# Issuing the down-projection weight loads from GpSimd's queue in place of SyncE's, in an eight-core transformer layer

## The chip, the cores and the metric

One Trainium2 chip, all 8 NeuronCores, one launch. Every core runs the same program on its own share of the tokens, and no core waits for another. The time is device microseconds of the slowest core.

## The reference

One post-norm transformer layer on x of shape (4, 4096, 2048): multi-head self-attention with 16 heads of 128, a projection, a residual and a layer norm, then a gated feed-forward network with 4-bit weights (I = 5632), an RMS norm of its result, a residual and a layer norm.

```python
x = _layernorm(x + attn(x, Wqkv, Wproj, bproj))
gate, up = x @ w_gate.T, x @ w_up.T        # w_* dequantized from fp4, group scales
y = (silu(gate) * up) @ w_down.T
y = y / sqrt(mean(y * y) + 1e-6)
x = _layernorm(x + y)
```

## The kernel before

The work is split by batch row and half of the sequence: each core has 2048 tokens. Three phases follow each other, each closed by waits for all of the one before.

Phase A computes Q, K, V and the attention, and between these dequantizes the packed weights into two scratch tensors in HBM, `wgu_scr` (gate and up) and `wdn_scr` (down, 5632 x 2048 bf16). Phase B does the projection, the residual and the first norm; it leaves h1 in HBM, once as f32 rows (`h_scr`) and once transposed (`h1T_scr`).

Phase C, in which the change lies, is the feed-forward network. It runs over 4 chunks (`ch`) of 512 tokens. A chunk has

- a gate-up stage: for each of 44 blocks `op` of 128 hidden units, 16 + 16 matmuls of 128x512 (L966 gate, L972 up) with the weight block `wbC` (1 MB, 4 buffers) and the chunk's transposed input `h1tc` (2 MB, 2 buffers); ScalarE does silu (L985), VectorE the product into `hffnT` (L994);
- two down stages (`pp` = 0, 1), each for a pair of 128-token tiles: for each of 44 blocks `ic`, 8 matmuls of 128x512 (L1040) with the weight block `wdC` (128 rows of 4 KB, 512 KB, 4 buffers) into all eight PSUM banks. All of `wdn_scr` is read once for each pair, 8 times in all;
- after each down stage an epilogue for each of its two tiles, on VectorE with two square roots on ScalarE: PSUM to `yC` (L1057), statistics, the residual with `h1rC` (L1103), the norm into `outfC` (L1136), and a store of 1 MB (L1145).

The order is that in which each engine's queue is written; there is no planner. SyncE's queue (SPq) issues all loads of phase C, in this order in a chunk: `h1tc` (L935), 44 times `wbC` (L947), then for each pair two loads of 1 MB `h1rC` (L1008) and 44 loads `wdC` (L1020). Each waits on SPq before it is issued: `wbC` number kc for the matmuls of kc-4 (L946), `h1rC` of a tile for the whole epilogue of the tile two before (`cyt`, L1007), `wdC` number kd for the last matmul of kd-4 (`dm`, L1019). So on SPq the loads `wdC` of pair 1 stand behind the epilogues of pair 0, and the loads of the next chunk stand behind the last `wdC` of this one.

GpSimd's queue (POOLq) issues in phase C only the 16 stores of `out` (L1145), each after its epilogue's last step. GpSimd computes nothing there.

TensorE starts the first block of a pair when `wdC` is there and the earlier pair's last tile has been copied out of PSUM (`cyev`); it starts a chunk's gate-up stage when the tile before the last one has been copied out. Its operation `op` waits for the product `op`-2 (`chm`), because gate and up use two pairs of banks in turn.

Of the kernel before, what the change touches and what calls it, by code (L numbers as in the profile page):

```python
# [111 lines left out]
def build_nc(cfg):  # L112
# [29 lines left out]
    d_wdn = nc.dram_tensor("wdn_scr", [I, H], BF16, kind="Internal").ap()  # L142
# [26 lines left out]
    with contextlib.ExitStack() as TOP:  # L169
        ET = TOP.enter_context  # L170
        sems = {n: ET(nc.semaphore(n)) for n in SEM_NAMES}
# [731 lines left out]
        with contextlib.ExitStack() as SC:  # L903
# [4 lines left out]
            wdC = [EC(nc.sbuf_tensor(f"wdC{i}", [128, H], BF16)) for i in range(4)]  # L908
# [10 lines left out]
            def phaseC(w: W):  # L919
# [10 lines left out]
                for ch in range(NTC):  # L930
                    if w.on("sync"):
                        s = w.eng
                        if ch >= 2:
                            s.wait_ge(sems["sCg"], w.m(f"cgc{ch-2}", "sCg"))
                        w.pinc(s.dma_start(out=h1tc[ch % 2][:],  # L935
                                           in_=d_h1T[:, ch * TOKCH:(ch + 1) * TOKCH]
# [3 lines left out]
                    for op in range(ITC):  # L940
                        par = op % 4
                        kc = ch * ITC + op
                        if w.on("sync"):
                            s = w.eng
                            if kc >= 4:
                                s.wait_ge(sems["sCg"], w.m(f"cg{kc-4}", "sCg"))  # L946
                            w.pinc(s.dma_start(out=wbC[par][:],  # L947
                                               in_=d_wgu[op, :, :].rearrange("(hc p) o -> p hc o",
                                                                             p=128)), "sCw", kc, 4)
# [3 lines left out]
                        par = op % 4  # L953
# [46 lines left out]
                    for pp in range(NPAIR):  # L1000
                        for tt2 in range(ntt2):
                            tt_abs = ch * TT + pp * 2 + tt2
                            parq = tt_abs % 2
                            if w.on("sync"):
                                s = w.eng
                                if tt_abs >= 2:
                                    s.wait_ge(sems["sCy"], w.m(f"cyt{tt_abs-2}", "sCy"))  # L1007
                                w.pinc(s.dma_start(out=h1r[parq][:],  # L1008
                                                   in_=d_h1[tt_abs * 128:(tt_abs + 1) * 128, :]),
# [3 lines left out]
                        for ic in range(ITC):  # L1013
                            kd = (ch * NPAIR + pp) * ITC + ic
                            par = ic % 4
                            if w.on("sync"):
                                s = w.eng
                                if kd >= 4:
                                    s.wait_ge(sems["sDm"], w.m(f"dm{kd-4}", "sDm"))  # L1019
                                w.pinc(s.dma_start(out=wdC[par][:],  # L1020
                                                   in_=d_wdn[ic * 128:(ic + 1) * 128, :]),
                                       "sDw", kd, 4)
                            else:
                                w.pnote("sDw", kd, 4)
                            for tt2 in range(ntt2):
                                for oc in range(NOC):
                                    if w.on("tensor"):
                                        t = w.eng
                                        if tt2 == 0 and oc == 0:
                                            w.pwait("sDw", kd, 4)  # L1030
                                            if ic == 0:
                                                t.wait_ge(sems["sCh"], w.c("sCh"))
                                                prev_last_tile = ch * TT + pp * 2 - 1
                                                if prev_last_tile >= 0:
                                                    t.wait_ge(sems["sCy"],
                                                              w.m(f"cyev{prev_last_tile}", "sCy"))
                                        lhs = (hffnT[:, ic, pp * 256 + tt2 * 128:
                                                     pp * 256 + (tt2 + 1) * 128] if TT > 1
                                               else hffnT[:, ic, 0:128])
                                        inst = t.matmul(pC[tt2 * 4 + oc][:, 0:OCW], lhs,  # L1040
                                                        wdC[par][:, oc * OCW:(oc + 1) * OCW],
                                                        start=(ic == 0), stop=(ic == ITC - 1))
                                        if tt2 == ntt2 - 1 and oc == NOC - 1:
                                            w.inc(inst, "sDm", 1)
                                    elif tt2 == ntt2 - 1 and oc == NOC - 1:
                                        w.note("sDm", 1)
                            w.snap(f"dm{kd}", "sDm")
                        for tt2 in range(ntt2):
                            tt_abs = ch * TT + pp * 2 + tt2
                            parq = tt_abs % 2  # L1050
                            if w.on("vector"):
# [4 lines left out]
                                for oc in range(NOC):  # L1056
                                    w.inc(v.tensor_copy(out=yC[:, oc * OCW:(oc + 1) * OCW],  # L1057
                                                        in_=pC[tt2 * 4 + oc][:, 0:OCW]),
# [4 lines left out]
                            if w.on("vector"):  # L1063
# [4 lines left out]
                                for st2 in range(NST):  # L1068
                                    last = v.bn_stats(out=sttC[:, st2, :],
                                                      in_=yC[:, st2 * STW:(st2 + 1) * STW])  # L1070
# [3 lines left out]
                                                     in_=sttC[:].rearrange("p a b -> p (a b)")),  # L1074
# [21 lines left out]
                            if w.on("vector"):  # L1096
# [13 lines left out]
                                for st2 in range(NST):  # L1110
                                    last = v.bn_stats(out=sttC[:, st2, :],
                                                      in_=r2[:, st2 * STW:(st2 + 1) * STW])
# [3 lines left out]
                                                     in_=sttC[:].rearrange("p a b -> p (a b)")),  # L1116
# [25 lines left out]
                            if w.on("gpsimd"):  # L1142
                                gp = w.eng
                                gp.wait_ge(sems["sCy"], w.c("sCy"))
                                w.pinc(gp.dma_start(out=d_out[tt_abs * 128:(tt_abs + 1) * 128, :],  # L1145
                                                    in_=outf[parq][:]), "sOut", tt_abs)
# [5 lines left out]
                if w.on("gpsimd"):  # L1152
                    for sname in ("sOut0", "sOut1"):
                        if w.c(sname) > 0:
                            w.eng.wait_ge(sems[sname], w.c(sname))

            run_phase(phaseC)

    return nc
# [65 lines left out]
```

## Time and profile before

| | us |
|---|---|
| median of the runs (2 runs, 6547.95 to 6553.09) | 6550.52 |
| profiled execution | 6540.59 |
| its span on the slowest core (core 1) | 6539.0 |
| spans of the eight cores | 6518.7 to 6539.0 |
| phase C begins at about | 4383 |

The profile is of core 1 of the profiled execution, and all times in rows are from its span's start. The mean granted clock of TensorE lies between 0.886 and 0.889 of its full speed on all cores. The profiled execution is 9.9 us below the median of the runs.

### The profile page before, as it was taken

Reading aid. Unit: us, or ns where it says so; the run is one execution under the profiler, and the core shown is the slowest. Engines: PE = TensorE matmul, PEld = TensorE weight load, DVE = VectorE, ACT = ScalarE, POOL = GpSimd, SP = SyncE. Lnnn points to the kernel's source line nnn. Section 1 sums busy time; section 2 is a strip of 40 time slices with the busy share of each in tenths; the row PEclk is TensorE's granted clock in tenths of the full one; section 3 lists DMA queues with packets and bytes.
Section 4 is the critical chain, followed back from the end, with each engine's and each line's share of the span. In section 5 each row is a group of like instructions: output and inputs, shape, how many; then the busy total and the mean of one; then the engine's idle time right before and its main releaser. Section 6 shows DMA issues by size and latency. Waiting matters only on the chain.

```text
span 6539.0 us, 82502 instructions; the slowest of 8 cores (6518.7 to 6539.0 us)
## 1 busy us (share of the span) xinstructions
PE 4668.7 (71%) x27520; PEld 2300.4 (35%) x27520; DVE 2362.7 (36%) x9935; ACT 2039.9 (31%) x2442; POOL 423.2 (6%) x510
## 2 busy tenths in 40 slices
PE   0587667876668776678766244449979979978995
PEld 0233443334443344433343122224434433433442
DVE  1234775347773367633576211111012112011003
ACT  0234765337663366733566111110000000000000
POOL 0000111001110011100111000000000000000000
PEclk9988898988988888999889677769989989989997
DMA  2333112341123321133111322234575466467565
GB/s 68 102 94 102 37 42 60 88 123 39 39 58 90 108 58 36 38 97 107 41 36 37 126 74 77 77 110 155 177 237 178 161 221 210 155 202 237 153 211 181
DMA packets 281821, 725.90 MB, mean 111 GB/s; under 512 B 26689, under 2 KB 43457, under 8 KB 271169
## 3 DMA queue, kind: packets, MB, share of 16 engines
q1 hardware_dynamic: 242306, 575.37, 28.2%
q0 software_dynamic: 39104, 145.27, 7.6%
q8 instruction: 231, 3.78, 0.2%
q14 instruction: 180, 1.47, 0.1%
HBM read 600.99 MB, written 119.54 MB: 110 GB/s over the span
## 4 chain that ended last, share of the span: by engine, by line
PE 47%; DMA 20%; DVE 15%; ACT 11%; issue 6%; POOL 0%; DVEq 0%; ACTq 0%; SPq 0%; POOLq 0%
DMA xf<-xt 10%; PE pC L966 9%; PE pC L972 9%; PE pC L1040 7%; ACT Pt L613 5%; PE pCV L514 5%; PE pCV L634 5%; PE pB L815 4%; PE pS L550 3%; DMA wdC<-wdn_scr 3%; PE pS L587 3%; DVE dqf L344 3%; DVE dq_bits L333 2%; ACT xbf L466 2%; DMA wq_st<-wqkvT 2%
## 5 line engine op out<-in xcount | busy, mean ns | idle before, releaser
L613 ACT ACTIVATE Pt<-pS,bias_c 128x1024 bf16<-128x1024 f32 x1024 | 1099.7, 1115 | 370.3 <-PE pS L587 359.4
L634 PE MATMUL pCV<-V_wave,Pt 128*128 128x129 bf16 x8192 | 706.5, 235 | 573.8 <-ACT Pt L613 315.1
L634 PEld LDWEIGHTS pCV<-V_wave,Pt 128*128 128x128 bf16 x8192 | 553.5, 105 | 1048.5 <-issue 1044.2
L1040 PE MATMUL pC<-wdC,hffnT 128*128 128x512 bf16 x2816 | 632.4, 383 | 197.4 <-DMA wdC<-wdn_scr 188.1
L514 PE MATMUL pCV<-wq_bf,xbf 128*128 128x512 bf16 x2048 | 521.7, 420 | 297.8 <-ACT V_wave L527 297.8
L966 PE MATMUL pC<-h1tc,wbC 128*128 128x512 bf16 x2816 | 652.1, 386 | 64.6 <-DVE hffnT L994 22.6
L587 PE MATMUL pS<-Q_wave,K_wave 128*128 128x512 bf16 x2048 | 676.7, 417 | 9.6 <-ACT K_wave L539 9.6
L344 DVE TENSOR_SCALAR dqf<-dq_bits,scf 128x128 bf16<-128x128 f32 x2112 | 667.3, 652 | 30.3 <-DVE dq_bits L333 1.4
L972 PE MATMUL pC<-h1tc,wbC 128*128 128x512 bf16 x2816 | 636.5, 379 | 0.0
L496 PE MATMUL pS<-xbf,wq_bf 128*128 128x512 bf16 x2048 | 455.5, 382 | 228.7 <-ACT xbf L466 218.8
L994 DVE TENSOR_TENSOR hffnT<-sGC,pC 128x512 bf16<-128x512 bf16 x176 | 121.1, 688 | 1099.1 <-ACT sGC L985 1099.1
L333 DVE TENSOR_TENSOR dq_bits<-dq_bits,dq_tmpB 128x128 int32<-128x128 int32 (+1 forms) x2176 | 480.2, 283 | 59.1 <-DVE dq_tmpB L324 1.8
L466 ACT CAST xbf<-xf 128x512 bf16<-128x512 f32 x512 | 313.9, 621 | 559.3 <-DMA xf<-xt 558.1
L318 DVE TENSOR_SCALAR dq_bits<-pk 128x128 int32<-128x128 int32 (+1 forms) x2176 | 356.5, 236 | 348.6 <-PE pTq L365 309.0
L1040 PEld LDWEIGHTS pC<-wdC,hffnT 128*128 128x128 bf16 x2816 | 269.7, 98 | 560.1 <-issue 265.5
L985 ACT ACTIVATE sGC<-pC 128x512 bf16<-128x512 f32 x176 | 105.1, 597 | 1075.8 <-PE pC L972 1072.9
L966 PEld LDWEIGHTS pC<-h1tc,wbC 128*128 128x128 bf16 x2816 | 278.8, 99 | 410.1 <-issue 88.5
L514 PEld LDWEIGHTS pCV<-wq_bf,xbf 128*128 128x128 bf16 x2048 | 213.7, 106 | 591.7 <-issue 405.0
L972 PEld LDWEIGHTS pC<-h1tc,wbC 128*128 128x128 bf16 x2816 | 275.6, 98 | 332.2
L496 PEld LDWEIGHTS pS<-xbf,wq_bf 128*128 128x128 bf16 x2048 | 200.2, 98 | 471.3 <-issue 241.4
L324 DVE TENSOR_SCALAR dq_tmpB<-pk 128x128 int32<-128x128 int32 (+1 forms) x2176 | 348.2, 228 | 0.0
L300 DVE TENSOR_SCALAR scf<-scb 128x16 f32<-128x16 f16 x88 | 16.0, 182 | 883.3 <-DMA pk<-gup 664.5
(73 smaller groups left out, 2694.7 us busy)
## 6 DMA issues: line engine op xcount, KB each, us to landing
wdC<-wdn_scr SPq DMA_DIRECT2D x352, 512.0 KB, 4.9
xf<-xt SPq DMA_DIRECT2D x512, 256.0 KB, 2.7
wgu_scr<-wtile POOLq DMA_DIRECT2D x176, 256.0 KB, 3.5
wdn_scr<-wtile POOLq DMA_DIRECT2D x80, 256.0 KB, 3.5
wp_st<-wprojT SPq DMA_DIRECT2D x16, 1024.0 KB, 4.8
xr<-xrows SPq DMA_DIRECT2D x16, 1024.0 KB, 7.2
h_scr<-h1f POOLq DMA_DIRECT2D x16, 1024.0 KB, 9.3
h1rC<-h_scr SPq DMA_DIRECT2D x16, 1024.0 KB, 7.9
```

The source lines that it names most:

```text
L318: lastw = v.tensor_scalar(out=bits_view(j), in0=pkt[:, c0:c0 + ncols], scalar1=m8, scalar2=28 - 4 * j, op0=ALU.bitwise_and, op1=ALU.logica ...
L333: last_or = v.tensor_tensor(out=bits_view(j), in0=bits_view(j), in1=dq_tmpB[:, jj * ncols:(jj + 1) * ncols], op=ALU.bitwise_or)
L344: last = v.tensor_scalar(out=dq_f[fifo][:, g * 128:(g + 1) * 128] .rearrange("p (i e) -> p e i", e=8), in0=bits3[:, :, g * 16:(g + 1) * 16 ...
L466: w.inc(sc.copy(out=xbf[xslot][:, hc, :], in_=xf32[:, kx % 2, :]), "sXC", 1)
L496: inst = t.matmul(pK(l), wq_bf[:, hc, (NL + l) * 128:(NL + l + 1) * 128], xbf[slot][:, hc, :], start=(hc == 0), stop=(hc == HC - 1))
L514: inst = t.matmul(pCV[st % 2][:, 0:NL * 128], xbf[slot][:, hc, st * 128:(st + 1) * 128], wq_bf[:, hc, 2 * NL * 128:3 * NL * 128], start=(h ...
L587: w.inc(t.matmul(pS2[(gti // 2) % 2][:, (gti % 2) * 512:(gti % 2) * 512 + QCH], K_wave[:, l, ti * 128:(ti + 1) * 128], Q_wave[:, l, sqc * ...
L613: w.inc(sc.activation(out=Pt[:, (gpi % 2) * 2:(gpi % 2) * 2 + 2, :], in_=pin, func=AF.Exp, bias=bias_c[:, 0:1], scale=NORM), "sSP", 1)
L634: inst = t.matmul(bank[:, off:off + 129], Pt[:, (gpi % 2) * 2 + tloc, qt * 128:(qt + 1) * 128], V_wave[:, l, ti, 0:129], start=(ti == 0), ...
L966: t.matmul(gb[:, 0:TOKCH], wbC[par][:, hc, 0:128], h1tc[ch % 2][:, hc, :], start=(hc == 0), stop=(hc == HC - 1))
L972: inst = t.matmul(ub[:, 0:TOKCH], wbC[par][:, hc, 128:256], h1tc[ch % 2][:, hc, :], start=(hc == 0), stop=(hc == HC - 1))
L1040: inst = t.matmul(pC[tt2 * 4 + oc][:, 0:OCW], lhs, wdC[par][:, oc * OCW:(oc + 1) * OCW], start=(ic == 0), stop=(ic == ITC - 1))
```

## The change

The 352 loads `wdC` and their waits move from SyncE's queue to GpSimd's. Source, destination, size, order among themselves, the semaphores that they raise and the condition that each waits for are unchanged.

```diff
                         for ic in range(ITC):
                             kd = (ch * NPAIR + pp) * ITC + ic
                             par = ic % 4
-                            if w.on("sync"):
-                                s = w.eng
+                            if w.on("gpsimd"):
+                                gp = w.eng
                                 if kd >= 4:
-                                    s.wait_ge(sems["sDm"], w.m(f"dm{kd-4}", "sDm"))
-                                w.pinc(s.dma_start(out=wdC[par][:],
-                                                   in_=d_wdn[ic * 128:(ic + 1) * 128, :]),
+                                    gp.wait_ge(sems["sDm"], w.m(f"dm{kd-4}", "sDm"))
+                                w.pinc(gp.dma_start(out=wdC[par][:],
+                                                    in_=d_wdn[ic * 128:(ic + 1) * 128, :]),
                                        "sDw", kd, 4)
```

On SPq the order of a chunk is then `h1tc`, 44 `wbC`, four `h1rC`, and the next chunk's `h1tc`. On POOLq it is, for each pair, 44 `wdC` and two stores of `out`.

## Rows read from the trace of the kernel before

**Rows 1.** The page: span, and the chain that ended last.
```profile
span 6539.0 us, 82502 instructions; the slowest of 8 cores (6518.7 to 6539.0 us)
PE 47%; DMA 20%; DVE 15%; ACT 11%; issue 6%; POOL 0%; DVEq 0%; ACTq 0%; SPq 0%; POOLq 0%
```
**Rows 2.** The page, group L1040: xcount | busy, mean ns | idle before, releaser.
```profile
L1040 PE MATMUL pC<-wdC,hffnT 128*128 128x512 bf16 x2816 | 632.4, 383 | 197.4 <-DMA wdC<-wdn_scr 188.1
```
**Rows 3.** Timeline of SPq, pair 1 into chunk 1: start, us, what, xcount.
```profile
4801.46 14.74 SPq L1008 DMA_DIRECT2D h1rC<-h_scr  x2
4816.60 86.85 SPq L1020 DMA_DIRECT2D wdC<-wdn_scr  x44
4903.50 0.43 SPq L935 DMA_DIRECT2D h1tc<-h1T_scr  x1
4904.10 303.43 SPq L947 DMA_DIRECT2D wbC<-wgu_scr  x44
```
**Rows 4.** Windows: length, busy of PE, PEld, DVE, ACT, POOL, clock, DMA share, GB/s.
```profile
4390.00:4410.00 20.00, 12.58 (x51) 5.35 (x52) 0.69 (x1) 1.88 (x2) 0.00 (x0) 0.73 0.85 274
4705.00:4785.00 80.00, 77.07 (x351) 33.25 (x350) 0.00 (x0) 0.00 (x0) 0.00 (x0) 1.00 0.80 263
4827.00:4911.00 84.00, 79.82 (x352) 33.73 (x352) 0.01 (x1) 0.00 (x0) 0.00 (x0) 0.98 0.84 279
```
**Rows 5.** Tile wdC from 4705 to 4800: TensorE's waits (us, times), landings.
```profile
  DMA wdC<-wdn_scr: 2.8, 5
DMA to landing us min/median/max: 4.0/4.9/6.4
```
**Rows 6.** Timeline, pair 0 into pair 1 of chunk 0.
```profile
4800.02 1.35 DVE L1136 TENSOR_SCALAR outfC<-r2C,aggC,scaC 128x2048 f32<-128x2048 f32 x1
4801.95 0.56 POOL L1145 DMA_DIRECT2D out<-outfC  x1 [423.53 <-DVE outfC L1136]
4816.37 0.55 POOL L1145 DMA_DIRECT2D out<-outfC  x1 [13.86 <-DVE outfC L1136]
4827.16 5.09 PE L1040 MATMUL pC<-wdC,hffnT 128*128 128x512 bf16 x14 [41.72 <-DMA wdC<-wdn_scr]
```
**Rows 7.** Tiles pk (POOLq loads, 128 KB) and wq_st (SPq, 192 KB), until 60: landings.
```profile
DMA to landing us min/median/max: 2.6/2.6/2.6
...
DMA to landing us min/median/max: 2.3/2.4/2.5
```
**Rows 8.** Tile ctx_t (POOLq, 512 KB), whole span: landings; timeline of one of them.
```profile
DMA to landing us min/median/max: 5.6/6.9/9.4
...
4168.74 0.53 POOL L881 DMA_DIRECT2D h_scr<-h1f  x1 [35.39 <-DVE h1f L872]
4173.79 0.55 POOL L768 DMA_DIRECT2D ctx_t<-ctx_scr  x1
```
**Rows 9.** Tile outfC: landings of stores at 4802 and 4816; at 4926 and 4941.
```profile
DMA to landing us min/median/max: 8.6/9.4/10.3
...
DMA to landing us min/median/max: 4.4/4.5/4.6
```
**Rows 10.** DMA queues from 4822 to 4825: packets, MB, share of 16 engines.
```profile
q0 software_dynamic: 104, 0.84, 65.7%
q1 hardware_dynamic: 108, 0.42, 33.9%
```
**Rows 11.** DMA packets from 4907 to 4912.
```profile
DMA packets 1807, 1.89 MB, mean 378 GB/s; under 512 B 11, under 2 KB 1790, under 8 KB 1807
```
**Rows 12.** Timeline, pair 1 of chunk 0 into the gate-up stage of chunk 1.
```profile
4917.43 6.45 PE L966 MATMUL pC<-h1tc,wbC 128*128 128x512 bf16 x16 [6.61 <-DVE scaC L1085]
4938.10 0.20 ACT L1127 ACTIVATE scaC<-scaC 128x1 f32<-128x1 f32 x1 [6.09 <-DVE scaC L1119]
4941.22 4.00 PE L966 MATMUL pC<-h1tc,wbC 128*128 128x512 bf16 x9 [6.98 <-DVE hffnT L994]
```
**Rows 13.** Timeline, start of phase C.
```profile
4397.42 5.35 PE L966 MATMUL pC<-h1tc,wbC 128*128 128x512 bf16 x16 [21.88 <-DMA wbC<-wgu_scr]
```

## The prediction

> **What bounds the kernel now.** I read the page first, then the windows of phase C, SPq's timeline, and last the timelines at the stage borders. The page shows the chain that ended last: TensorE 47%, DMA 20% [rows 1]. The change touches only phase C, some 2155 of 6539 us, and in it one group of the page matters, L1040: 2816 matmuls, 632.4 us busy, 197.4 us idle before them, 188.1 of these waiting for `wdC` [rows 2]. That looks like a loading problem worth 188 us. It is mostly not. At the start of pair 1 TensorE is idle for 41.72 us in one piece [rows 6]; there are four such starts, 4 x 41.72 = 166.9 us, so only 188.1 - 166.9 = 21.2 us are waits inside the eight down stages. Of the 41.72 us, all but the last 10.8 pass while VectorE works at the two epilogues: `out` of the second tile is issued at 4816.37 and TensorE starts at 4827.16 [rows 6]. The load waits for that epilogue on either queue, on SPq through `h1rC` of the second tile, on POOLq through the store of `out`.
>
> Inside a down stage the kernel is close to two limits at once. In pair 0 TensorE is busy for 77.07 of 80 us, at full clock, while the DMA engines are busy 0.80 and move 263 GB/s, and VectorE, ScalarE and GpSimd are idle [rows 4]. One block (8 matmuls) takes 77.07/351 x 8 = 1.757 us. A buffer is asked for when block kd-4 is done and must be there three blocks later, after 5.27 us; the landing takes 4.0/4.9/6.4 us (minimum, median, maximum), and five late ones cost 2.8 us [rows 5]. SPq issues 0.09 us after the event it waited for (4800.02 + 1.35 = 4801.37, issue at 4801.46) [rows 3, 6]. So the median load has 5.27 - 4.9 - 0.09 = 0.28 us to spare. That small number is what the change plays with.
>
> **Part 1, the loads' loop on POOLq (steady part).** Two terms grow.
> - From the event to the issue: on the same event POOLq issues at 4801.95, 0.49 us after SPq [rows 3, 6].
> - From issue to landing: undisturbed, 128 KB on POOLq land in 2.6 us, 192 KB on SPq in 2.4 [rows 7]. 64 KB less are 0.17 us at 378 GB/s [rows 11], so SPq would need 2.2 for 128 KB, and POOLq is 0.4 us slower.
>
> Together 0.89 us, against 0.28 to spare. The loop of four buffers gives (1.757 + 0.58 + 5.3)/4 = 1.91 us for a block, where the same sum before gave (1.757 + 0.09 + 4.9)/4 = 1.69, that is, TensorE's own 1.757 ruled, plus 21.2/352 = 0.06 for late ones: 1.82. The difference is 0.09, and I take 0.10, since loads that are late now count in full: 352 x 0.10 = **35 us**. Lower bound: the engines get slack as the loop slows; if landings fall to the minimum, 4.0 + 0.4, the loop needs 1.68 and nothing shows: 0. Upper bound: nothing to spare and no relief, 0.89/4 = 0.22, x 352 = 78 us. The 0.55 us that GpSimd needs to issue one [rows 6] is well under a block, so its queue doesn't run full. What stands behind a waiting load on POOLq is only the stores of `out`, which come after the pair anyway.
>
> **Part 2, what SPq does with its freedom.** SPq no longer waits for `dm`. Once the second epilogue of pair 0 is over, it issues `h1rC`, and at once `h1tc` and four `wbC` of the next chunk, which before came at 4903.50 and 4904.10, three blocks ahead of the end of pair 1 [rows 3]. The other 40 wait for the gate-up stage, as before. That is 2.1 + 4.2 = 6.3 MB thrown at the engines just as pair 1 starts with empty buffers, in three chunks (the last has no next). If the flood took the engines for itself, it would hold them 6.3 MB / 378 GB/s [rows 11] = 16.6 us, the upper bound for a chunk. It won't get all: between 4822 and 4825, with both queues full, 104 packets of POOLq and 108 of SPq went through, one for one, although the ones were 8 KB and the others 4 [rows 10]. `h1tc` comes in 1 KB packets and `wbC` in 2 KB (the 1790 of 1807 packets of rows 11 are the former), `wdC` in 4 KB, so `wdC` gets 4/5 and then 2/3 of 378 GB/s: 302 and 252. A block then takes 2.08 us at 252 GB/s for as long as 4.2 MB need at 126 GB/s, 33 us: 16 blocks x (2.08 - 1.92) = 3 us. But there is also standing in line: stores that come just behind a 1 MB load land in 8.6 to 10.3 us, with no such load in 4.4 to 4.6 [rows 9]. If each `wdC` waits 4.9 us like that, a block takes (1.757 + 0.58 + 10.2)/4 = 3.1 us; the flood then moves at 378 - 524/3.1 = 210 GB/s and is over in 30 us, 10 blocks x 1.2 = 12 us. Between 3 and 12 I take 8: 3 x 8 = **24 us** (bounds 9 and 50).
>
> A rule of the Trainium skill bears on this: "DMA: Bandwidth & Descriptors", section "Queues, rings and completion order", says that an engine alternates between rows only at whole packets, typically 9 to 17 descriptors. The trace's one-for-one count speaks for single descriptors [rows 10]. By the page, with 17 of 2 KB at 378/16 GB/s each, 1.5 us would be added to each load where one for one adds 0.7, as an estimate some 5 us a chunk in place of 3; both lie inside what I took.
>
> **Part 3, what early `wbC` gains.** At the border to chunk 1 TensorE is idle for 6.61 us before the first gate matmuls and 6.98 us before the third operation [rows 12]. The early loads can take some 4 us off the first idle time: PSUM has to be copied out anyway. But the third operation waits for VectorE's product of the first, which waits for a silu, which stands on ScalarE's queue behind the square root of the last epilogue, at 4938.10 [rows 12]. That chain begins with the end of pair 1 and doesn't move. What the first wait gives back the second takes: **0 us**; were it kept, 3 x 4 = 12 us.
>
> **Part 4, starts.** At the start of phase C TensorE waits 21.88 us for `h1tc` and the first `wbC` [rows 13]. POOLq now issues four `wdC`, 2.1 MB, at the same moment, and at 4 KB against 1 KB they go first. At 274 GB/s [rows 4] that is 7.7 us if all of it is ahead, 0 if none; I take **6 us**, once. Later chunks prefetch these four as GpSimd comes free, beside a gate-up stage which needs them only 300 us later. At the start of pair 1 the first `wdC` is issued at 4816.37 + 0.55, 0.3 us later than by SPq (4816.60), and goes behind the store of `out` on its own ring, not behind `h1rC`. Ahead of it are the same 2 MB; `h1tc` mixes in. I take **+1 us** for each of four: 4 us. Lower bound: clear of `h1rC`, store and load land 1.0 + 1.57 MB / 378 GB/s + 0.8 = 6 us after the issue, a gain of 4.3 each, 17 us. (The 1.0 and 0.8 split what 4.4 us for the store leaves beside 2.8 us of moving.) Upper bound 3 each, 12.
>
> **The sum.** 35 + 24 + 0 + 6 + 4 = 69 us. On the profiled execution's 6540.6 us that is 6609.6. The median of the runs lies 9.9 us above the profiled execution, so I predict 6620 us, 1.1% more.
>
> **Rivals.**
> - *Hidden.* The relief of part 1 is full and the flood is passed by: 0 + 9 + 0 + 6 - 17 = -2, with the 12 us of part 3 and nothing for the start -20. Time 6530 to 6570. For it: the minimum landings. Against it: 0.28 us to spare. A gain of over 2% (131 us) can't be had: all waits for `wdC` inside stages (21), the starts of pair 1 down to zero (4 x 10.8 = 43) and part 3 (12) are 76 us together.
> - *Slow landings (slower by over 2%).* The nearest load by form is `ctx_t` on POOLq, also 128 rows of 4 KB: 5.6/6.9/9.4 us [rows 8]. With 6.9 the loop takes (1.757 + 0.58 + 6.9)/4 = 2.31 us, 0.49 more than 1.82, x 352 = 172 us, with the other 34: 6757 us. Against it: `ctx_t` is issued 5 us after a 1 MB store on its own ring [rows 8], and `wdC` follows only its like. It decides from (131 - 34)/352 = 0.28, a loop of 2.10 us, a landing of 6.1.
> - *Starved.* The flood takes its full 16.6 us a chunk, 50 where I took 24: 6646 us. It stays within 2%.
>
> **Chances.** Forecast, with the starved case in it (+20 to +131): 0.64. Hidden (-20 to +20): 0.21. Slow landings: 0.15. The range goes from 6545, nearly all of the hidden case's middle, to 6695: 78 + 50 + 8 + 12 = 148 us, all upper bounds together. About 2% is what a measurement of this kernel can tell from no change: faster 0.01, within 0.85, slower 0.14.
>
> **What would show it.** In the changed profile: landings of `wdC` at 5.0 to 5.6 us on POOLq, and 0.58 us from event to issue; pair 0 of each chunk 84 to 86 us in place of 80, with many waits of half a microsecond; pair 1 of chunks 0 to 2 longer than pair 1 of chunk 3 by about 8 us, in its first 40; `h1tc` issued just after 4816; TensorE's wait at the start of phase C near 28 us; the third operation of the next gate-up stage still 30 us after the end of pair 1. Pair 0 still at 80 us would refute part 1. I would be wrong upward if GpSimd's issues came late in a row, and downward if the store no longer stood ahead of the first load.

## The result: 1.4% slower, and the profile after

| | us |
|---|---|
| runs of the changed kernel | 6637.4 to 6645.2 |
| profiled execution's span, slowest core | 6635.8 (before: 6539.0) |
| ratio to the runs before, 95% interval | 1.014, 1.0121 to 1.0158 |

1.014 times the 6550.5 that the prediction stood on is 6642 us. Six of the 11 executions of the changed kernel and seven of the 10 of the kernel before were lengthened by a lower TensorE clock on one or both dies (in those of the changed kernel 0.76 to 0.86 in the mean of a core, where it is 0.88 to 0.89 otherwise), which is why the medians over all of them are 6785.76 after and 6766.09 before; the other times and ratios here are of executions, cores and stages without that.

The page of the changed kernel, with the groups that answer to [rows 1] and [rows 2], and the landings of `wdC`:

```profile
span 6635.8 us, 82502 instructions; the slowest of 8 cores (6607.5 to 6635.8 us)
PE 44%; DMA 23%; DVE 15%; ACT 10%; issue 6%; POOL 0%; DVEq 0%; ACTq 0%; SPq 0%; POOLq 0%
L1040 PE MATMUL pC<-wdC,hffnT 128*128 128x512 bf16 x2816 | 648.3, 386 | 264.8 <-DMA wdC<-wdn_scr 254.7
wdC<-wdn_scr POOLq DMA_DIRECT2D x352, 512.0 KB, 5.1
```

TensorE's wait for `wdC` went from 188.1 to 254.7 us, and its own group from 632.4 to 648.3, in part because it restarts at a lower clock more often (in pair 1 of chunks 0 to 2, 28 matmuls of a stage last more than 0.45 us each, where it was 11). The chain has moved 3% of the span from TensorE to DMA.

A stage's length is read from the tile `wdC`: first and last start of its 352 matmuls, the wait for the load (us, times), the landings. Changed kernel, core 0, pair 0 and pair 1 of chunk 0, and pair 1 of chunk 3:

```profile
L1040 PE MATMUL pC<-wdC,hffnT x352: 376/379/380, 4713.4 to 4797.9; 128*128 128x512 bf16 x176
  DMA wdC<-wdn_scr: 5.3, 11
DMA to landing us min/median/max: 4.3/4.9/5.9
...
L1040 PE MATMUL pC<-wdC,hffnT x352: 375/379/632, 4841.9 to 4939.8; 128*128 128x512 bf16 x176
  DMA wdC<-wdn_scr: 58.4, 16
...
L1040 PE MATMUL pC<-wdC,hffnT x352: 376/379/635, 6507.1 to 6593.6; 128*128 128x512 bf16 x176
```

They last 84.5, 97.9 and 86.5 us. Read in this way for every stage of every core, the means are as follows; "idle ahead" is here the time from the start of the last matmul of pair 0 to the first of pair 1, 0.4 us more than TensorE's gap.

| mean over cores, us | before | after | difference, x how often |
|---|---|---|---|
| TensorE's wait ahead of phase C's first matmul | 19.7 | 25.6 | 6 |
| pair 0 | 79.5 | 85.6 | 6.1 x 4 = 24 |
| idle ahead of pair 1 | 41.6 | 44.1 | 2.5 x 4 = 10 |
| pair 1, chunks 0 to 2 | 83.6 | 100.8 | 17.2 x 3 = 52 |
| pair 1, chunk 3 | 82.4 | 87.2 | 5 |
| end of pair 1 to the next chunk's first `wdC` matmul | 325.0 | 325.0 | 0 |
| last matmul to the end of the span | 37.1 | 42.1 | 5 |
| sum | | | 102 |

The mean span of the eight cores grew by 93 us (6529.7 to 6622.9), that of the slowest by 97. The phases ahead, which the change doesn't touch, ended 8 us earlier in this one execution (in the mean, TensorE's wait ahead of phase C begins at 4364.4 in place of 4372.3), and this moment scatters by 10 us and more from core to core.

The border between pair 0 and pair 1, timeline of the changed kernel (answers to [rows 6]):

```profile
4827.22 1.35 DVE L1136 TENSOR_SCALAR outfC<-r2C,aggC,scaC 128x2048 f32<-128x2048 f32 x1
4829.02 0.43 SPq L935 DMA_DIRECT2D h1tc<-h1T_scr  x1
4829.14 0.54 POOL L1145 DMA_DIRECT2D out<-outfC  x1 [13.88 <-DVE outfC L1136]
4829.66 22.05 SPq L947 DMA_DIRECT2D wbC<-wgu_scr  x2
4829.66 2.10 POOL L1020 DMA_DIRECT2D wdC<-wdn_scr  x4
4841.93 3.57 PE L1040 MATMUL pC<-wdC,hffnT 128*128 128x512 bf16 x8 [43.70 <-DMA wdC<-wdn_scr]
```

`h1tc` and `wbC` of the next chunk are issued in the same microsecond as pair 1's first `wdC`. What they meet there is seen in the windows of the changed kernel, pair 0, then the first 36 us and the rest of pair 1 (columns as in [rows 4]):

```profile
4713.00:4798.00 85.00, 79.02 (x352) 32.76 (x352) 0.25 (x1) 0.00 (x0) 21.13 (x40) 1.00 0.73 247
4843.00:4879.00 36.00, 25.52 (x100) 9.69 (x99) 0.00 (x0) 0.00 (x0) 6.34 (x12) 0.91 1.01 331
4880.00:4938.00 58.00, 53.55 (x239) 22.16 (x238) 0.00 (x0) 0.00 (x0) 14.79 (x28) 1.00 0.81 264
```

For 36 us the DMA engines are full (1.01) at 331 GB/s, and TensorE does 100 matmuls where some 164 would fit at the 77.07/351 us each of [rows 4]. From 4880 on it runs nearly as in pair 0.

### The profile page after: what moved, and what is told of

The parts are those of the page before. It is cut to its first block, busy times and chain, and to the rows that moved or that the text cites. A ratio compares the mean times of both kernels' runs of the same rounds, so it can differ in the third digit from the quotient of the medians.

```text
span 6635.8 us, 82502 instructions; the slowest of 8 cores (6607.5 to 6635.8 us)
## 1 busy us (share of the span) xinstructions
PE 4674.9 (70%) x27520; PEld 2294.5 (35%) x27520; DVE 2362.1 (36%) x9935; ACT 2039.1 (31%) x2442; POOL 614.7 (9%) x862
## 3 DMA queue, kind: packets, MB, share of 16 engines
q1 hardware_dynamic: 191618, 390.80, 19.7%
## 4 chain that ended last, share of the span: by engine, by line
PE 44%; DMA 23%; DVE 15%; ACT 10%; issue 6%; POOL 0%; DVEq 0%; ACTq 0%; SPq 0%; POOLq 0%
DMA xf<-xt 10%; PE pC L966 9%; PE pC L972 9%; DMA wdC<-wdn_scr 6%; PE pC L1040 5%; ACT Pt L613 5%; PE pCV L634 5%; PE pCV L514 4%; PE pB L815 4%; PE pS L550 3%; PE pS L587 3%; DVE dqf L344 3%; DVE dq_bits L333 2%; ACT xbf L466 2%; DMA wq_st<-wqkvT 2%
## 5 line engine op out<-in xcount | busy, mean ns | idle before, releaser
L1040 PE MATMUL pC<-wdC,hffnT 128*128 128x512 bf16 x2816 | 648.3, 386 | 264.8 <-DMA wdC<-wdn_scr 254.7
L1040 PEld LDWEIGHTS pC<-wdC,hffnT 128*128 128x128 bf16 x2816 | 267.2, 99 | 645.9 <-issue 365.4
L390 POOL DMA_DIRECT2D wgu_scr<-wtile x176 | 180.5, 1026 | 2155.2 <-ACT wtile L375 2040.5
L1020 POOL DMA_DIRECT2D wdC<-wdn_scr x352 | 185.9, 529 | 1755.8 <-PE pC L1040 1743.7
```

The costliest lines, as they stand in the source:

```text
L1040: inst = t.matmul(pC[tt2 * 4 + oc][:, 0:OCW], lhs, wdC[par][:, oc * OCW:(oc + 1) * OCW], start=(ic == 0), stop=(ic == ITC - 1))
```

## The experiments

Two sources of cost were on the table: a longer loop for each load (part 1 of the prediction) and the next chunk's early loads (part 2). The rivals were that the store ahead on the same ring, the empty buffers, or a lower rate of the software queue were to blame. Stage times are means over cores, as above, and those of pair 1 are of chunks 0 to 2 where nothing else is said. The edits are abridged; the comments in them and `...` are mine.

**Hold the next chunk's loads back.** On SyncE, ahead of `h1tc` in the changed kernel:

```diff
+                        if ch >= 1:
+                            s.wait_ge(sems["sDm"], w.m(f"dm{ch * NPAIR * ITC - 5}", "sDm"))
                         w.pinc(s.dma_start(out=h1tc[ch % 2][:],
```

> The changed kernel, but SyncE holds back the next chunk's h1tc and wbC loads with a wait for the same matmuls (the fifth block before the end of pair 1) that held them back in the kernel before. Theory A (the early loads of the next chunk take the DMA engines from wdC at the start of pair 1): pair 1 of chunks 0 to 2 falls from 98 to 102 us to that of chunk 3, about 87, and the idle time ahead of it by 1 to 2; the span falls by 3 x 14 = 42 us to about 6590. Theory B (pair 1 is long because the wdC loads stand behind a store of 1 MB on their own ring and start with empty buffers): pair 1 stays near 100 us and the span near 6635. Both: pair 0 stays at 84 to 87 us.

Pair 1 of chunks 0 to 2 falls from 100.8 to 91.9 us, the idle time ahead of it from 44.1 to 42.3; pair 0 stays (85.7). Spans are 6594 to 6615 us on the four cores of one die, the ratio to before is 1.0112 (1.0068 to 1.0155). Core 0, pair 1 of chunk 0, and SyncE's timeline:

```profile
L1043 PE MATMUL pC<-wdC,hffnT x352: 376/379/631, 4851.9 to 4942.2; 128*128 128x512 bf16 x176
...
4930.33 0.37 SPq L938 DMA_DIRECT2D h1tc<-h1T_scr  x1
```

Theory A holds for 8.9 us. Of the 17.2 us that pair 1 had grown, chunk 3, which has no next chunk, shows 4.8 (82.4 to 87.2) as the longer loop's, so 12.4 were the next chunk's, and 3.5 of these remain. It does not come down to this run's chunk 3, 88.3: at the same point in the kernel before, `h1tc` stood behind the last `wdC` on one ring, and here the last four `wdC` share the engines with it. Order on one ring had protected them: this is the reading that fits, no run takes it apart further.

**The same held back to the middle.** As above with `ITC - 25`, so that they go at block 20.

> The changed kernel, with the next chunk's h1tc and wbC held back until block 20 of pair 1. Theory (what costs is that 6.3 MB pass beside a stream that has 0.3 us to spare, whenever they pass): pair 1 of chunks 0 to 2 stays at 98 to 102 us, and only the idle time ahead of it falls, from 44 to 42. Rival (what costs is their meeting the empty buffers at the start of pair 1): pair 1 falls to about 90 us.

Pair 1 takes 103.2 us, no less than with the loads at its start (100.8); the idle time ahead falls to 42.6, and the span is 6651 us. Core 5, SyncE's timeline and pair 1 of chunk 0:

```profile
4880.47 0.37 SPq L938 DMA_DIRECT2D h1tc<-h1T_scr  x1
...
L1043 PE MATMUL pC<-wdC,hffnT x352: 376/379/634, 4841.1 to 4946.7; 128*128 128x512 bf16 x176
```

So empty buffers are not what makes them expensive: 6.3 MB beside a stream with next to nothing to spare cost the same at its start and in its middle. The rival falls.

**Only pair 0 on GpSimd.**

```diff
-                            if w.on("sync"):
+                            if w.on("gpsimd" if pp == 0 else "sync"):
```

> Only the wdC loads of pair 0 are issued by GpSimd, those of pair 1 by SyncE as before (with semaphores of their own). Theory A (a longer loop on GpSimd's queue, and early loads of the next chunk, are two separate costs): pair 0 takes 85 to 86 us as in the changed kernel, pair 1 is back at 82 to 84 in all chunks because SyncE stands at its own waits again; start of phase C 4 us later; span about 4 x 6 + 4 + 2.5 = 30 us over the kernel before, 6570. Theory B (the length of a down stage follows from something that both pairs share, such as HBM): pair 1 stays above 84. GpSimd's drain at the end took 2.7 us before with 510 DMAs and 7.7 with 862; if it goes by their number it takes about 5.2 here with 686.

Core 0, pair 0 and pair 1 of chunk 0:

```profile
L1042 PE MATMUL pC<-wdC,hffnT x352: 376/379/379, 4718.5 to 4803.6; 128*128 128x512 bf16 x176
  DMA wdC<-wdn_scr: 6.5, 11
DMA to landing us min/median/max: 3.6/5.0/6.2
...
L1042 PE MATMUL pC<-wdC,hffnT x352: 376/379/634, 4845.2 to 4927.3; 128*128 128x512 bf16 x176
DMA to landing us min/median/max: 3.7/4.9/5.7
```

Means 84.8 and 83.4 us: pair 0 pays, pair 1 doesn't, side by side in one run. Landings are alike on both queues (5.0 and 4.9). What differs is the issue. Taken from the trace as the time from the start of the block's last matmul to the issue of the load that waits for it, the median is 0.92 us on GpSimd and 0.46 us on SyncE, in this kernel and in the two compared. The span is 6576, 37 us over before, where 30 was expected: the start of phase C costs 6 us again, not 4, and GpSimd's drain at the end takes 7.99 us, not 5.2.

**ScalarE's queue, a second hardware queue.**

```diff
-                            if w.on("sync"):
+                            if w.on("scalar"):
```

> All wdC loads are issued from ScalarE's queue, a second hardware queue; SyncE is as free as in the changed kernel. Theory A1 (the steady loss of 6 us a stage is GpSimd's late issue, 0.49 us after the event): pair 0 is back at 79 to 81 us, while pair 1 of chunks 0 to 2 still suffers from the next chunk's early loads and takes 95 or more. Theory A2 (the steady loss comes from having the loads on another ring than SyncE's): pair 0 stays at 85. The first loads of pair 0 are issued only after the last silu, so 3 to 5 us of waiting appear at its start; those of pair 1 no longer wait for the store, some 3 us gained in the idle time ahead of it.

The issue comes 0.46 us after the event, as on SyncE. From block 8 on, the other 36 blocks of pair 0 take 65.6 us, as on SyncE (65.5), where GpSimd's queue needs 70.8 (means over the six cores whose matmul records are complete), so the steady loss is gone. The 2.6 us by which pair 0 is longer than before (82.1) lie in its first eight blocks, for which the first loads are issued only behind the last silu. Pair 1 of chunk 3 takes 86.3 us, 3.9 over before, also in its first eight blocks: there the second `h1rC` is issued 2 us after the first `wdC` and passes beside it. Pair 1 of chunks 0 to 2 takes 103.2 us: the early loads cost on a hardware queue what they cost on GpSimd's. And the idle time ahead of pair 1 falls to 33.8, since on this queue nothing waits for the last step of the epilogue and no store stands ahead. Span 6605 us. Core 3:

```profile
4829.98 0.46 SPq L935 DMA_DIRECT2D h1tc<-h1T_scr  x1
4830.62 32.03 SPq L947 DMA_DIRECT2D wbC<-wgu_scr  x2
4832.74 5.65 PE L1040 MATMUL pC<-wdC,hffnT 128*128 128x512 bf16 x16 [33.55 <-DMA wdC<-wdn_scr]
```

**Six buffers on GpSimd, next chunk held back.**

```diff
-            wdC = [... for i in range(4)]
+            wdC = [... for i in range(6)]
-                            par = ic % 4          # and kd >= 4, dm{kd-4}
+                            par = kd % 6          # and kd >= 6, dm{kd-6}
```

> As the first kernel of this set (next chunk's loads held back), with six wdC buffers in place of four, so that a load is asked for five blocks ahead and not three. Theory A (the steady loss is latency: 0.58 us to issue and 4.9 to land against 5.27 us): TensorE no longer waits inside a stage, pair 0 and pair 1 take 77 to 78 us each, the eight stages together 8 x 9 = 72 us less than in the changed kernel on top of the 42 of held-back loads: span about 6520. Rival (the software queue carries less in a second): the stages stay at 84 to 87 us, span about 6590.

Pair 0 takes 76.0 us and pair 1 78.0, on the queue that needed 85.6. Window of pair 0, chunk 2, core 0:

```profile
5988.00:6064.00 76.00, 75.96 (x352) 34.26 (x350) 0.00 (x0) 0.00 (x0) 20.09 (x38) 1.00 0.77 263
```

TensorE is busy for 75.96 of 76 us with the DMA engines at 0.77. GpSimd's queue carries the stream at full speed once a load is asked for five blocks ahead, so the steady loss was latency and not the queue's rate. (The spans of this run, 6737 to 7000 us at a mean granted clock of 0.80, can't be compared; the two means are of stages at full clock.)

**Six buffers on SyncE, nothing else** (the kernel before with the same edit).

> The kernel before with six wdC buffers in place of four, nothing else. Theory (four buffers on SyncE were 0.28 us from stalling at the median and stalled for the late loads): pair 0 falls from 79.4 to 76 to 77 us, pair 1 from 83 to 78, span 6539 - 4 x 3 - 4 x 5 = about 6507. Rival: no change in the stages.

Pair 0 takes 75.8 and pair 1 78.0 us, spans of four cores 6480 to 6500. As expected; four buffers had been short in the kernel before too, by 3.7 us in pair 0 and 5.6 in pair 1.

**Order: the residual's loads behind the weights.** The kernel before, the two `h1rC` loads of pair 1 moved into the loop:

```diff
+                            if pp > 0 and ic == 20:
+                                h1r_loads()       # the two L1008 loads, not ahead of ic 0
```

> The kernel before (all loads on SyncE), with one change of order: the two h1rC loads of pair 1, which wait for the epilogues of pair 0, are issued behind wdC number 20 of pair 1 in place of ahead of wdC number 0. Theory (of the 41.7 us idle ahead of pair 1, PSUM binds TensorE only until the second tile is copied out, some 18 us after the end of pair 0; the rest is the load that stands behind h1rC on the queue): the idle time falls to 18 or 19 us, four times 23, and the span by 90 us to about 6445. Rival (the wait is the epilogue's in another way, or the time comes back as slower loads and a halved clock in pair 1): the idle time falls but pair 1 grows by as much, span above 6500.

The span is 6493.6 us. The timeline of core 7, and pair 1 of chunk 0:

```profile
4808.73 10.56 PE L1045 MATMUL pC<-wdC,hffnT 128*128 128x512 bf16 x40 [18.45 <-DVE yC L1062]
...
L1045 PE MATMUL pC<-wdC,hffnT x352: 376/379/634, 4808.7 to 4902.5; 128*128 128x512 bf16 x176
  DMA wdC<-wdn_scr: 12.0, 12
```

The releaser ahead of pair 1 is now the copy out of PSUM, and the idle time is 19.0 us in place of 41.6. So 22.6 us of each such wait had been the queue's order, as the theory says. But pair 1, over all chunks, grew from 83.3 to 93.0, which is nearly half of the gain: 2 MB of `h1rC` go through the ring ahead of block 20's load, beside the stores. The truth lies between theory and rival: the span fell by 45 us, not by 90.

**Both** (six buffers and that order):

> The order of the run before this one, and six wdC buffers on SyncE's queue. Theory: stages at TensorE's own 76 to 78 us in place of 79.4 and 83.6, so 8 x 4.5 = 36 us less again: span about 6410. Rival: HBM or the engines limit a stage at 79 us or more and the buffers bring under 10 us.

Runs take 6442 to 6457 us, ratio 0.9817 (0.9736 to 0.9898), an interval that reaches to both sides of a 2% gain. That is 30 us and more above what was expected; in chunk 3, on the four cores at full clock there, pair 0 takes 75.8 and pair 1 84 to 85, not 78.

**Spread them:** one `h1rC` at block 14, the other at 28.

> All loads on SyncE, six wdC buffers, and the two h1rC loads of pair 1 issued one by one behind wdC number 13 and number 27 of pair 1 (in the earlier run both together behind number 19). Theory (pair 1 took 84 us there because 2 MB of h1rC pass through the ring ahead of the next wdC, and once that is spread, six buffers cover it): pair 1 falls to 77 to 80 us, the idle time ahead of it stays at 19, pair 0 at 76; span 4 x 5 = 20 us under the 6442 to 6457 of that run, about 6430. Rival (pair 1 is long because the epilogues of pair 0 run beside it): pair 1 stays at 84 us.

Pair 0 takes 75.8 us, and the span falls to 6432.1 us, as expected. Pair 1, over all chunks, falls to 81.5 us only, not to the 77 to 80 forecast: spreading the loads brings some 3 us of the 6 to 7 over 78, and what the rest is, the epilogues beside it or `h1rC` still, no run separates. A second set of the same kernel:

> The kernel with six buffers and spread h1rC loads once more, for an interval: by its first profile (6432 us span) against 6539 before, the ratio should lie between 0.980 and 0.985. If it is above 0.985, the gain seen there was partly the chip's scatter.

The four runs of both sets take 6433.8 to 6440.9 us, against 6541.3 to 6575.6 for the six of the kernel before beside them: 0.982 by their means, the low half of what was expected. This version is 1.8% faster than the kernel before and some 3% faster than the changed one, which was not run beside it.

**GpSimd's queue with nothing in the way.** The changed kernel, next chunk held back, and the stores of pair 0 moved to SyncE:

> The changed kernel with the next chunk's loads held back, and the stores of out of pair 0 moved from GpSimd's to SyncE's queue, so that no wdC load stands behind a store that waits for an epilogue (four buffers). Theory: the idle time ahead of pair 1 falls from 44 to 18 or 19 us as in the reordered kernel on SyncE; the stages keep GpSimd's longer loop, 85 to 88 us; end and start as in the changed kernel. Span 6594 - 4 x 23 = about 6500, so 50 us behind the reorder on SyncE: the queue alone, without its side effects, costs that. Rival: with the loads free, GpSimd's queue is no worse than SyncE's, span about 6450.

The idle time is 19.0 us, pair 0 85.4, pair 1 98.9 (chunk 3: 94.0), spans 6519 to 6551 on one die. With the loads on SyncE and `h1rC` at block 20 it was 79.9 and 93.5 (chunk 3: 91.5), spans 6469 to 6494. So with no `wdC` load behind a wait for an epilogue in either, the version on GpSimd is 51 us longer in the mean span (6534 against 6483), as forecast: 22 in pair 0, 19 in pair 1, 5 each at the start and the end of phase C. Not all of it is the queue's alone, since the orders differ: here the `h1rC` of pair 1 pass on SyncE's queue beside its first blocks, there on the same ring at block 20.

**The last stage alone on GpSimd.**

> The kernel before with the wdC loads of the very last stage alone (chunk 3, pair 1) on GpSimd's queue. Theory: that stage takes 86 to 88 us in place of 82, nothing else changes ahead of it. GpSimd's drain at the end, 2.68 us with 510 DMAs, 7.99 with 686 and 7.66 with 862: if any wdC load on the queue brings the long drain, it is 7.5 us or more here with 554; if it goes by the number of DMAs in some steps, it can lie anywhere between.

That stage takes 88.1 us against 82.4, at the upper end of the 86 to 88 forecast, and all others are as before (79.9 and 83.3). The drain takes 5.45 us, the span is 6554 us.

## Why the prediction was right and where it failed

The direction and the ratio came out as forecast: 1.1% more was predicted and 1.4% measured. Two things failed: the level that the sum was added to, and the size of most terms of the sum.

**The level.** The forecast of a time, 6620 us in a range from 6545 to 6695, rests on the step "on the profiled execution's 6540.6 us that is 6609.6", plus 9.9. It takes the level of two executions of the kernel before, at a mean granted clock of 0.886 to 0.889, for that of all, and puts the term for a lower clock at nothing, without a reason. The measured median over all executions is 6785.76, 91 us above the range, and the kernel before, run again beside it, has 6766.09 in place of 6550.5, for the lower granted clock told of with the result. On the level that the prediction stood on the result is 6642 us, inside the range. Why the clock was lower stays open.

**The terms of the sum,** 69 us forecast against about 102:

- **Part 1, the loop: 35 us forecast, about 44 measured** (24 in pair 0, and 4.8 in each of four pairs 1, as chunk 3 shows it clean). The mechanism is shown, by pair 0 and pair 1 of one run, by ScalarE's queue and by the six buffers, but two of its numbers were wrong, one each way. The step from event to issue was right: 0.49 us forecast, 0.46 measured in the loop. The 0.4 us for a slower landing, drawn from a 128 KB and a 192 KB load at the start of the kernel [rows 7], is mostly not there: the median in pair 0 is 4.85 us before and 5.00 after, over the six cores with complete records. And the 0.28 us to spare were not there either. The sum took 1.757 us for a block, where one takes 1.73 when nothing waits (75.8 us for 351 of 352 matmuls, with six buffers), and it left out that a matmul starts 0.14 us after its load has landed: so it is for the blocks that waited, in both kernels. From the start of the last matmul of block kd-4, block kd is due after 3 x 1.73 + 0.22 = 5.41 us, and the median load of the kernel before needs 0.46 + 4.85 + 0.14 = 5.45. With nothing to spare, a quarter of the whole 0.46 + 0.15 = 0.61 us should show in a block, 0.15; over blocks 8 to 43 of pair 0 a block went from 1.82 to 1.97 us. It is a mean: of 864 such blocks 128 waited before and 265 after, and the median block is 1.73 us in both.
- **Part 2, the flood: 24 us forecast, 17.2 - 4.8 = 12.4 us for each of three chunks, 37 measured.** Right in place and kind, and at the "stand in line" end, 12, of what was worked out; I had taken 8, between it and the 3 of one-for-one sharing, so this is the term most under its size. There `wdC` was to land in 4.9 + 0.4 + 4.9 = 10.2 us; from 4843 to 4876 the landings of the changed kernel are

```profile
DMA to landing us min/median/max: 6.3/9.2/12.5
```

  The rule of the Trainium skill named there ("DMA: Bandwidth & Descriptors", "Queues, rings and completion order") gave some 5 us a chunk; the run shows 12.4, so neither packets one for one nor whole packets alone account for it.
- **Part 3, early `wbC`: 0 forecast, 0.0 measured.** The first gate matmuls start 3.2 us after pair 1 in place of 7.2, and the third operation waits for the same 4 us more, and for up to 3 us more where the first 16 gate matmuls, after the shorter pause, run at the higher clock (3.61 us in place of the 6.45 of [rows 12]); it still starts 30.8 us after the last `wdC` matmul of pair 1, as before. Timeline of the changed kernel, chunk 0 into 1 (answers to [rows 12]):

```profile
4942.97 3.61 PE L966 MATMUL pC<-h1tc,wbC 128*128 128x512 bf16 x16 [2.81 <-DVE yC L1057]
4967.44 0.20 ACT L1127 ACTIVATE scaC<-scaC 128x1 f32<-128x1 f32 x1 [6.08 <-DVE scaC L1119]
4970.56 4.85 PE L966 MATMUL pC<-h1tc,wbC 128*128 128x512 bf16 x11 [13.62 <-DVE hffnT L994]
```

- **Part 4, starts: 6 + 4 us forecast, 6 + 10 measured.** At the start of phase C TensorE waits 25.6 us in the mean over cores, where it was 19.7: the 6 us forecast. The single cores of the two pages, 25.83 on core 0 and 21.88 on core 1 [rows 13], would show 4. Ahead of pair 1 it was 2.5 us each, not 1: 10 in place of 4. With the next chunk held back 0.7 remain (42.3), so the larger part is `h1tc` mixing in. (Two slips change nothing here: of 4.4 us less 2.8 of moving 1.6 are left for the split into 1.0 and 0.8, and all upper bounds together end at 6698, not 6695.)
- **Not foreseen: 5 us at the very end,** a term that the sum put at nothing. GpSimd's drain, its last instruction before the engines' closing semaphores, takes 7.66 us in place of 2.68, on every core alike.

The rival of slow landings (0.15) is out: median landings of 4.9 to 5.1 us. The hidden case is out too. "Starved" was nearest for part 2, but even it, at 50, would have overstated. The sentence that only 10.8 of 41.7 us ahead of pair 1 belong to the load, "all but the last 10.8 pass while VectorE works at the two epilogues", is true of the queue as it stands, and misled: I called 76 us all that could be gained from these waits. The reorder took 22.6 us from each of four, 90 us, before half was given back to `h1rC`, because TensorE needs the copy out of PSUM and not the epilogue's end.

## What to carry over

With a fixed number of buffers, compare the time from "buffer free" to "data there" with the time the engine takes for the blocks between: if the difference is a few tenths of a microsecond, a queue that reacts half a microsecond later costs, with four buffers, a quarter of that in the mean block, and here two more buffers were worth more than the choice of queue (76.0 us for pair 0 on GpSimd's with six, 79.5 on SyncE's with four). Count the time from landing to the first matmul in it, and take the block's time where nothing waits. Before moving a stream off a queue, ask which other transfers that queue was holding back, since a wait in the old order can be what kept them out of the way. And of a load that is late, ask what stands ahead of it on its queue, and whether that really has to come first.

## What the hardware showed

- GpSimd's queue reacts 0.46 us later to the same kind of event than SyncE's or ScalarE's (0.92 against 0.46 and 0.46 from the start of the last matmul), in every trace looked at. 512 KB loads in pair 0 then land in 5.00 us (median), against 4.85 and 4.90.
- A matmul that waited for its load starts 0.14 us after the landing (0.25 in a few cases), on all three queues.
- GpSimd's drain at the end took 2.68 us with 506 DMAs issued on its queue, 5.45 with 550, 7.99 with 682, 7.50 with 850 and 7.66 with 858 (the numbers in the expectations count four other instructions too). Within a kernel it is the same on all cores. It grows and then stops growing; what it depends on was not settled.
- Two streams from two queues share the engines to the harm of the one that is waited for, whichever kind of queue it is on (100.8 and 103.2 us for pair 1, on GpSimd's and ScalarE's); the same transfers on one ring behind the stream cost 1.2 (83.6 in chunks that have them, 82.4 in the one that has not).
